# A quarter of the last dense node pair beside the fourth dense slot pass, and the third score pass in one part

## The reference, cut to what matters

```python
def _sage_layer(h, edge_src, edge_dst, W, b):
    msg_sum = jax.ops.segment_sum(h[edge_src], edge_dst, num_segments=n)
    deg = jax.ops.segment_sum(jnp.ones_like(edge_dst, dtype=h.dtype), edge_dst, num_segments=n)
    m = msg_sum / jnp.maximum(deg, 1.0)[:, None]
    return jax.nn.relu(jnp.concatenate([h, m], axis=1) @ W + b)
h = _sage_layer(h, edge_src, edge_dst, W1, b1)
h = _sage_layer(h, edge_src, edge_dst, W2, b2)
x = _layernorm(x + _L3_gnn_ref(x, src, dst, ...), axis=-1)
```

## Time and profile before

| | |
|---|---|
| median of 3 runs | 5069.83 us (5068.57 to 5076.53) |
| profiled execution | 5069.27 us, span 5067.3 us |
| PE / PEld busy | 3921.8 (77%) / 2869.7 (57%) us |
| DVE / ACT / POOL busy | 3812.1 (75%) / 3449.9 (68%) / 3019.2 (60%) us |
| mean granted TensorE clock | 0.910 |
| third score pass, first gathers of its two parts | at 2729.06 and 2933.55 us |
| first gathers of the five dense passes | at 3505.92, 3779.68, 4040.47, 4303.13 and 4560.63 us |

### The profile page before, as it was taken

One profiled execution on the slowest core, in us unless ns is written; L12 is line 12 of the kernel. 1 busy time (PEld: TensorE's weight loads), 2 busy tenths in 40 slices (PEclk: granted clock), 3 DMA queues, 4 the chain that ended last, 5 costly groups with the idle time before them and its releaser, 6 DMA issues. The chain is left out here.

```text
span 5067.3 us, 107533 instructions
## 1 busy us (share of the span) xinstructions
PE 3921.8 (77%) x23992; PEld 2869.7 (57%) x23992; DVE 3812.1 (75%) x14850; ACT 3449.9 (68%) x11317; POOL 3019.2 (60%) x2914
## 2 busy tenths in 40 slices
PE   2999999566997799994998974997876676665554
PEld 1666766344775455773555752444766565665554
DVE  5899999676998787897886966997758787444433
ACT  0899999554886576894776863887878787333332
POOL 2888888475552122761224462887757676767777
PEclk9999999787998899997999997998999899997666
DMA  1556666587997576994777984675766665543332
GB/s 62 164 185 198 200 194 190 177 283 250 348 351 254 175 242 207 350 363 155 241 240 240 336 298 144 226 226 169 232 203 209 190 208 185 156 146 116 93 100 70
DMA packets 606698, 1061.18 MB, mean 209 GB/s; under 512 B 109736, under 2 KB 130874, under 8 KB 606508
## 3 DMA queue, kind: packets, MB, share of 16 engines
q1 hardware_dynamic: 524780, 920.61, 53.1%
q0 software_dynamic: 81728, 138.51, 10.6%
HBM read 608.75 MB, written 453.92 MB: 210 GB/s over the span
## 5 line engine op out<-in xcount | busy, mean ns | idle before, releaser
L2534 POOL DMA_INDIRECT got_c<-table,src_row x980 | 931.5, 951 | 387.8 <-issue 292.9
L1428 POOL DMA_INDIRECT src_got_s<-table,src_row x588 | 554.6, 943 | 439.1 <-issue 93.5
L2566 PE MATMUL bank<-pick_c,got_c 128*128 128x128 f32 x1960 | 334.0, 324 | 360.1 <-DMA got_c<-table,src_row 293.0
L2076 PE MATMUL bank<-w_all,dt_m 128*128 128x512 f32 x1176 | 568.7, 600 | 34.7 <-DMA dt_m<-delta_t 33.1
L2566 PEld LDWEIGHTS bank<-pick_c,got_c 128*128 128x128 f32 x1960 | 289.6, 227 | 402.1 <-issue 245.8
L2050 POOL TENSOR_TENSOR part_m<-part_m,half_sum_m 128x512 f32<-128x512 f32 x98 | 158.7, 1619 | 580.7 <-DVE half_sum_m L2283 580.7
L1601 ACT ACTIVATE z_s<-z_s,shift_s,dev_s 128x128 f32<-128x128 f32 x1080 | 443.9, 485 | 2.5 <-DVE shift_s L1739 1.3
L791 PEld LDWEIGHTS bank<-w_mean,ht 128*128 128x128 f32 x2352 | 312.1, 193 | 142.9 <-issue 142.9
L2590 PE MATMUL bank<-w_c,agg_c 128*128 128x128 f32 x1960 | 367.9, 313 | 5.6 <-ACT agg_c L2711 5.3
L2711 ACT COPY agg_c<-bank 128x512 f32<-128x512 f32 x245 | 142.6, 582 | 328.3 <-DVE bank L1914 280.2
L788 PE MATMUL bank<-bias,first_row 128*128 128x512 f32 x588 | 321.9, 629 | 38.0 <-ACT ht L851 14.3
(11 more groups left out here) (352 smaller groups left out, 11913.3 us busy)
## 6 DMA issues: line engine op xcount, KB each, us to landing
table<-rows SPq DMA_DIRECT2D x294, 256.0 KB
x_s<-table SPq DMA_DIRECT2D x270, 256.0 KB
x_c<-table SPq DMA_DIRECT2D x245, 256.0 KB
table<-z_s SPq DMA_DIRECT2D x196, 256.0 KB
table<-z_c SPq DMA_DIRECT2D x196, 256.0 KB
table<-mid_s SPq DMA_DIRECT2D x172, 256.0 KB
own_rows_s<-table SPq DMA_DIRECT2D x147, 256.0 KB
pick_t_s<-picks_t SPq DMA_DIRECT2D x147, 256.0 KB
```

Source lines behind the costliest of these rows:

```text
L1428: nc.gpsimd.indirect_dma_start(out=src_got[r][:, g, :], out_offset=None, in_=tables[l].rows, in_offset=bass.IndirectOffsetOnAxis(ap=src_ro ...
L2076: nc.tensor.matmul(b_h[k % n_h][:, :], dt[b.slot][:, k, :], w_all[:, l, :, :].rearrange("p h d -> p (h d)"), start=True, stop=True).then_i ...
L2534: nc.gpsimd.indirect_dma_start(out=got[r][:, g, :], out_offset=None, in_=t_in.rows, in_offset=bass.IndirectOffsetOnAxis(ap=src_row[:, t:t ...
L2566: ins = nc.tensor.matmul(b_sum[r][:, k * P:(k + 1) * P], got[b.slot][:, k, :], pick[r][:, k, :], start=k == 0, stop=sage, skip_group_check ...
```

## The change

The third score pass becomes one part: all 49 edge batches with one node batch a turn. Its node batches are 0, 2, ... 96. The fourth dense pass gets the argument nodes, with the offset 1: node batches 1, 3, ... 49. The first dense pass keeps its node batches: spare is 49, as 2 (nb - middle) + 1 was. Batch 49 is handled twice after the change, as it was before.

```diff
-        middle = (nb + 1) // 2
+        spare = nb // 2 * 2 + 1
         third = (t[6], t[7], t[8], (io["L3_gnn_W1"][0:D, :], io["c_L3_gnn_b1"]), (io["L3_gnn_W2"][0:D, :], io["b_L3_gnn_b2"]))
-        edge_scores(2, third[3], third[4], *third[0:3], 0, middle)
-        edge_scores(2, third[3], third[4], *third[0:3], middle, nb, True)
+        edge_scores(2, third[3], third[4], *third[0:3], 0, nb, True)
         softmax(2)
         attend(2)
-        convolve(0, "gcn0", False, t[3], t[4], None, (io["L1_gnn_W1"],), io["b_L1_gnn_b1"], third + (2 * (nb - middle) + 1,))
+        convolve(0, "gcn0", False, t[3], t[4], None, (io["L1_gnn_W1"],), io["b_L1_gnn_b1"], third + (spare,))
         convolve(1, "gcn0", True, t[4], t[5], t[3], (io["L1_gnn_W2"],), io["b_L1_gnn_b2"])
         convolve(2, "gcn1", True, t[5], t[6], t[5], (io["L2_gnn_W"],), io["b_L2_gnn_b"])
-        convolve(3, "sage", False, t[6], t[7], None, (io["L3_gnn_W1"][D:, :], io["L3_gnn_W1"][0:D, :]), io["b_L3_gnn_b1"])
+        convolve(3, "sage", False, t[6], t[7], None, (io["L3_gnn_W1"][D:, :], io["L3_gnn_W1"][0:D, :]), io["b_L3_gnn_b1"], third + (1,))
```

## The result

The changed kernel takes 5253.1 us (median of 4 runs, 5251.2 to 5262.1), the kernel before 5070.3 in the same job: a ratio of 1.0362, 95% interval 1.0347 to 1.0378. The prediction had 5223 with a range of 5160 to 5295 and 0.91 on slower. One execution of the kernel before, beside the first four experiments, took 12997 us with no cause seen; the ratios leave it out.

A forecast was written before the change was run, and what follows sets the result against it. A row of passes with barriers between; in the fourth dense pass written instruction order makes TensorE and ScalarE take turns. 5069.3 - 71.1 (score pass) + 157.5 (chain) + 12.4 (tail) + 55.4 (clock) = 5223.5 us, range 5160 to 5295.

The forecast's parts named there:

- Bound and mechanism: Fourth dense pass: room in busy time, but written order makes TensorE and ScalarE take turns; two turns 16.46 us, before 9.87.
- Third score pass: One part of 49 single-batch turns at 5.456 us an interval gives back 71.1 us.
- Rival 3: Waits in the fourth dense pass as forecast, but DMA holds the score pass to 7.54 us a turn: 5323.5 us; chance 0.04.
- The chain: Fourth dense pass: TensorE and ScalarE waiting on each other make 48 turns take 395.0 us, 157.5 more at full clock.
- the clock: Fourth dense pass: mean granted TensorE clock 0.81 adds 55.4 us; 0 at 1.00, 121.7 at 0.66.
- The signs: Fourth dense pass: products wait for ACT agg_c, gathers for TensorE's sums; odd turns 9 to 10 us, even 7.5 to 8.5.
- Rival 2: TensorE's clock stays on the lower level for the whole fourth dense pass: 236 us instead of 55, total 5404; chance 0.04.
- Tail: Fourth dense pass, last product's end to next gather: takes the first pass's 17.2 us instead of 4.8, 12.4 more.
- Start: Fourth dense pass: four small weight loads and one more bias matmul at its start cost 0 within 2 us.
- First dense pass: It takes the same node batches, 49, 51, ... 97, before and after: 0 us.
- Rival 1: Node steps hide in the fourth dense pass, which keeps its 4.94 us turn: 5010.6 us, faster by 58.7; chance 0.08.

The follow-up runs named there:

- the short loads: The changed kernel with node batch loads of 32 of 512 columns after the third score pass's first turns (node rows come out wrong): 5258.5 us.
- The filler run: The changed kernel with idle TensorE matmuls added in the fourth dense pass, three behind each hidden product, two behind each middle transposes: 5162.0 us.
- the run with the normalise behind the sums: The changed kernel with ScalarE's normalise of the node rows moved behind the copies of the sums in the fourth dense pass: 5188.5 us.

## Why the prediction was right

**Bound and mechanism.** Right. The fourth pass had room in busy time and none in order. ScalarE's copies behind the relu made the two engines take turns; moving that one part took 230 us off with the same work. The rule of the Trainium skill that I leaned on ("TensorE: Matmul & The Clock Gate", section "Architectural detail": ScalarE and VectorE are strict first-in first-out) agrees with the trace. ScalarE was idle 6.76 us until the middle transposes were done and copied the sums after that, at 4518.89. All that this copy needed was there much earlier: VectorE had added what is carried at 4505.09, as its timeline in the changed kernel shows.

```profile
4505.09 0.17 DVE L1914 TENSOR_TENSOR bank<-bank,carried_c 128x8 f32<-128x8 f32 x1
```

**Third score pass.** Predicted 71.1 us back, measured 70.0 at the start of the next dense pass, or 72.5 counted from the pass's own first gather of tail rows, which came at 2718.46 before and at 2720.94 after. The turn was 5.49 us instead of 5.456. Rival 3 (the DMA share of 1.00 holds it to 7.54) did not come, and by the short loads that share does not set the 5.49 either.

**The chain.** From the own transposes of turn 3 to the last product's end in the changed kernel:

```profile
4248.94 0.60 PE L2576 MATMUL bank<-ident,x_c 128*128 128x128 f32 x4
...
4726.31 0.64 PE L2593 MATMUL bank<-w_c,own_c 128*128 128x128 f32 x2
```

That is 4726.95 - 4248.94 = 478.0 us for 48 turns, where 236.96 stood. The prediction had 395.0 less 0.54 for the chain and 55.4 for the clock, 449.9. The filler run separates the two: at clock 1.00 the same 48 turns take 382.0 us, 12 less than my 394.5. Of these 12 us, 9 are the pair (16.10 for 16.46), and the rest the short pairs at both ends. The clock's share is then 478.0 - 382.0 = 96 us where I had 55: this is the term that was mis-sized, by 41 us. The two misses have opposite signs, and so only 28 us are left of them; that the total came as close as 0.6% is in part luck.

The signs by which I would have known the chain came out in kind: all 48 products of turns 3 to 50 wait for ACT agg_c, and the gathers wait for TensorE's sums. The lengths given there for single turns did not: the odd one of the pair above takes 10.61 us (9 to 10 forecast) and the even one 9.84 (7.5 to 8.5), by the clock.

**Why the clock's term was too small.** I took a mean of 0.81 and spread it evenly over TensorE's work. The mean was 0.76. And it is not spread evenly: in the pair shown the lower level (1.2 GHz) falls on what comes behind the gaps. Both products of the pair run at it, 3.58 and 3.43 us (4509.99 to 4513.57, and 4519.54 to 4522.97) instead of 1.79 each; that alone is 3.4 of the 4.35 us that the pair (20.45) is longer than 16.10. TensorE had stood idle 3.78 and 2.87 us just before them. In one number: 9.48 us of TensorE's pace (16.10 less ScalarE's 6.62) took 20.45 - 6.62 = 13.83, as if the clock had been 0.69 (an estimate, with ScalarE's links taken as unchanged). Rival 2, all at the lower level, did not come.

**Tail.** Predicted 12.4; the last product ends at 4726.95, the next gather is at 4742.94, so 16.0 us instead of 4.8: plus 11.2. **Start.** Put at 0 within 2: turn 3 begins 15.3 us after the first gather (15.8 before). **First dense pass.** 0: 273.3 against 273.8.

**Rival 1**, the node steps hidden at 5010.6, is what the order of the gcn passes gives: 5021.4 when it is written so. It was a claim about an order that the kernel did not have, and as one about room it was right.

## What to carry to other kernels

When work is added to a software pipeline, room in busy time is only half of the check: walk one turn of each engine's written order and look for a producer that now stands behind a wait on its own consumer's turn. In such a chain price each link start to start from rows of a pass that runs the same steps; the chain at full clock came out 3% too long (394.5 for 382.0). Price the clock first with the links behind long gaps at the lower level, and not by a mean; here that is right for gaps of 3.78 and 2.87 us that came in every pair, and too dear for those of the run with the normalise behind the sums.

## What the runs showed of the hardware

- Idle work can make a chain faster. 25 fillers of 2.74 us and 24 of 1.88, together 114 us of matmuls, fill gaps and take 91 us off the total, the granted clock going from 0.76 to 1.00.
- A step of 1.54 us taken off the path was worth 2.9 us per pair of turns, as the gap before the next product shrank from 3.78 to 2.26 us and the mean clock rose from 0.76 to 0.84. With gaps of 2.26 and 2.87 to 2.95 us in every pair, some pairs ran all at the higher level (14.60 us) and some mostly at the lower (19.05).
- A DMA share of 1.00 is no proof of a bound: with 13% less traffic (339 to 296 GB/s) the turn stayed at 5.5 us and the share fell only to 0.91.
- Passes that no edit touches move by some us from profile to profile. The third score pass's first gather of tail rows stands between 2717.7 and 2727.2 us in the ten kernels profiled, and the first dense pass takes 272.8 to 277.1 us. With one profile of each kernel, no run here says why, nor whether the kernel or the execution makes the difference. It is of the size of what one node batch costs (6.9 us), so such an effect has to be read inside a pass, at the rows where it arises.
